# Local attention scores and value weighing on 64-row halves of the array, in a fused four-block network

## What is computed

```python
def local_attention(q, k, v):            # 16 heads of 64, windows of 32 tokens
    bk2, bv2 = (look(bk), look(bv))      # the window before and the own one: 64 keys
    sim = einsum('bhwie,bhwje->bhwij', bq, bk2) * QK_SCALE
    sim = where(mask, -finfo.max, sim)
    attn = softmax(sim, -1)
    out = einsum('bhwij,bhwje->bhwie', attn, bv2)
def ffn_layer(x, g, bln, W1, b1, W2, b2):
    hg = layernorm(x, g, bln) @ W1 + b1
    a, gate = split(hg, 2, -1)
    return a * gelu(gate) @ W2 + b2
for i in range(6):
    x = attn_layer(shift_tokens(x), ...) + x    # l2norm and rotary of q and k, output by Wo
    x = ffn_layer(shift_tokens(x), ...) + x
```

## Time and profile before

| | |
|---|---|
| three executions | 2566.87 to 2575.82 us, median 2572.84 |
| the profiled execution, its own time | 2572.18 us |
| its span, first to last instruction | 2570.4 us |
| stage 2 in the span | about 165.75 to 1949.57 us |
| one step of stage 2, steady | 36.48 us, the same within 0.02 us from step 5 on |
| busy shares of the span | PE 92%, DVE 69%, ACT 63%, POOL 62% |
| mean granted TensorE clock | 0.967 |

### The profile page before, as it was taken

One profiled execution on the slowest core, in us unless ns is written; L12 is line 12 of the kernel. 1 busy time (PEld: TensorE's weight loads), 2 busy tenths in 40 slices (PEclk: granted clock), 3 DMA queues, 4 the chain that ended last, 5 costly groups with the idle time before them and its releaser, 6 DMA issues.

```text
span 2570.4 us, 57541 instructions
## 1 busy us (share of the span) xinstructions
PE 2377.1 (92%) x22655; PEld 1629.8 (63%) x22655; DVE 1767.5 (69%) x2708; ACT 1615.4 (63%) x3162; POOL 1603.1 (62%) x931
## 2 busy tenths in 40 slices
PE   5669999999999999999999999999997888889998
PEld 3435666666666666666666666666665666656665
DVE  2348778777777777777877787778764888843232
ACT  1227777777777777777777777777773666643332
POOL 1039888888888888888888888888862222201111
PEclk8879999999999999999999999999997999989999
DMA  4002223322233222322232222322223000000000
GB/s 108 0 14 62 53 59 73 72 62 58 62 80 71 55 60 68 75 62 59 56 80 70 60 55 64 78 68 56 56 54 100 1 1 2 1 1 5 5 4 5
DMA packets 77196, 127.11 MB, mean 49 GB/s; under 512 B 24948, under 2 KB 48770, under 8 KB 76930
## 3 DMA queue, kind: packets, MB, share of 16 engines
q1 hardware_dynamic: 76930, 123.42, 20.6%
HBM read 26.56 MB, written 1.07 MB: 11 GB/s over the span
## 4 chain that ended last, share of the span: by engine, by line
PE 61%; DVE 13%; ACT 13%; issue 9%; POOL 3%; SPq 0%; DMA 0%; ACTq 0%; POOLq 0%; DVEq 0%
PE bank L527 8%; PE bank L563 7%; PE bank L604 7%; PE obank L584 6%; PE bank L618 6%; PE bank L813 5%; DVE qk L1211 2%; PE bank L538 2%; PE obank L823 2%; PE bank L823 2%; ACT kT L926 2%; ACT kT L925 2%; DVE mx L1367 2%; DVE sh L1364 2%; PE lnbank L548 2%
## 5 line engine op out<-in xcount | busy, mean ns | idle before, releaser
L1211 DVE TENSOR_TENSOR qk<-bank,tab 128x1024 f32<-128x1024 f32 x384 | 468.9, 1221 | 247.6 <-ACT qk L900 247.6
L1521 POOL TENSOR_TENSOR qk<-qk 128x1024 f32<-128x1024 f32 x192 | 454.3, 2366 | 251.9 <-DVE qk L1211 251.9
L1525 POOL TENSOR_TENSOR rn<-n2m,cst 128x16 f32<-128x16 f32 x192 | 562.5, 2930 | 16.0
L527 PE MATMUL bank<-wqk,xs 128*128 128x512 f32 x768 | 399.8, 602 | 4.0 <-DMA xs<-Z 1.3
L1529 POOL TENSOR_TENSOR qk<-qk,rn 128x1024 f32<-128x1024 f32 x192 | 365.2, 1902 | 28.1 <-POOL rn L1525 0.9
L900 ACT ACTIVATE qk<-bank 128x512 f32<-128x512 f32 x384 | 228.4, 595 | 210.0 <-PE bank L527 208.4
L538 PEld LDWEIGHTS bank<-cst,qk 128*128 128x128 f32 x1536 | 192.2, 141 | 210.6 <-issue 186.4
L1533 POOL TENSOR_TENSOR lnr<-lnv,cst 128x2 f32<-128x2 f32 (+1 forms) x88 | 66.2, 753 | 382.1 <-DVE lnv L1105 382.1
L538 PE MATMUL bank<-cst,qk 128*128 128x128 f32 x1536 | 231.7, 274 | 7.5 <-POOL qk L1529 7.5
L1218 DVE TENSOR_REDUCE n<-qk 128x16 f32<-128x1024 f32 x192 | 232.1, 1209 | 0.0
L912 ACT COPY vp<-lnbank 64x512 f32<-64x512 f32 x384 | 224.8, 585 | 9.4
(11 more groups left out here) (195 smaller groups left out, 4432.5 us busy)
## 6 DMA issues: line engine op xcount, KB each, us to landing
vp<-vp SPq DMA_DIRECT2D x672, 130.0 KB, 2.4
wqk<-in_L_ffn_Wqkv SPq DMA_DIRECT2D x24, 256.0 KB, 3.1
wv<-in_L_ffn_Wqkv SPq DMA_DIRECT2D x6, 512.0 KB, 3.6
wo<-in_L_ffn_Wo SPq DMA_DIRECT2D x6, 512.0 KB, 4.2
xs<-Z SPq DMA_DIRECT2D x48, 64.0 KB, 2.0
xs<-Z SPq DMA_DIRECT2D x48, 63.8 KB, 2.0
kT<-rel_by_distance SPq DMA_DIRECT2D x1, 2048.0 KB, 8.0
vp<-in_L_ffn_w SPq DMA_DIRECT2D x1, 2048.0 KB, 13.6
```

What stands on the lines that cost most here:

```text
L527: nc.tensor.matmul(bank[s % 2][:, :], xs[:, odd, WIN + r * P:WIN + r * P + P], wqk[:, lo:lo + 512], start=True, stop=True).then_inc(p_full, 1)
L1211: tt(qk[:, both, :].rearrange("p o (h d) -> p o h d", d=DH), heads(bank[c % 2][:, :]).unsqueeze(1).broadcast_to([P, 2, PAIRS, DH]), table. ...
L1521: tt(direct, direct, swapped, ALU.add).then_inc(sum_done, 1)
L1525: tt(rn[:, m % 2, :], n2m[:, :], const("mhalf"), ALU.pow).then_inc(rn_done, 1)
```

## The change

- `scores` and `weigh` work on the two 64-row halves of the array: for each head pair, window and half there is one matmul of 64 contraction rows and 32 stationary columns against 64 (scores) or 65 (weigh) columns. 32 matmuls in place of 16, and each half writes its own bank (`sbank` has two, `obank` has two).
- kT and vp lose their zero halves; ACT copies keys and values with one 128-row instruction in place of two of 64 rows. The memsets at the start and the spreading DMAs move half the bytes.
- `weigh` and `divide_out` move from the even slot to the odd slot after it, `divide_out` ahead of `norms`. `turn_out` and `take_out` move from the odd to the next even slot (the fourth one into slot 0 of the next step); `turn_out` now writes `obank[:, 1]`. `turn_probs` becomes the last operation of PE's odd slot. `seed` follows `shift_scores` at once.
- All three `hidden` blocks use bank 2, so block c waits for `gate` of block c-1.
- Stage 3's bias moves to two tiles, and stage 4's second weight gets a tile of its own.

```diff
-HD_BANK = (2, 4, 2)
...
-                    sp.wait_ge(v_done, 8 * t + 2)
+                    sp.wait_ge(v_done, 4 * t + 1)
...
                 for q in range(4):
                     for w in range(4):
                         lo = r * P + w * WIN
-                        keys = kT[:, 4 * g + q, :, lo:lo + 2 * WIN].rearrange("p o (s j) -> p o s j", s=2)
-                        mm = nc.tensor.matmul(s[WIN * w:WIN * w + WIN, q * P:q * P + P], qT[:, 4 * g + q, lo:lo + WIN],
-                                              keys if w % 2 else keys[:, :, ::-1, :], start=False, stop=True,
-                                              skip_group_check=True)
+                        for o in range(2):
+                            own = slice(64 * o, 64 * o + 64)
+                            keys = kT[own, 4 * g + q, lo:lo + 2 * WIN].rearrange("p (s j) -> p s j", s=2)
+                            mm = nc.tensor.matmul(sbank[WIN * w:WIN * w + WIN, o, q * DH:q * DH + DH],
+                                                  qT[own, 4 * g + q, lo:lo + WIN],
+                                                  keys if w % 2 else keys[:, ::-1, :], start=False, stop=True,
+                                                  skip_group_check=True)
...
                 wait(pe, ao_done, 4 * i + k)
+                wait(pe, ot_done, 4 * i + k)
                 for q in range(4):
                     for w in range(4):
-                        mm = nc.tensor.matmul(obank[WIN * w:WIN * w + WIN, q // 2, (q % 2) * VB:(q % 2) * VB + VB],
-                                              pT[:, k % 2, q * P + w * WIN:q * P + w * WIN + WIN],
-                                              vp[:, 4 * r + w, 4 * g + q, :], start=True, stop=True)
+                        for o in range(2):
+                            own = slice(64 * o, 64 * o + 64)
+                            mm = nc.tensor.matmul(obank[WIN * w:WIN * w + WIN, o, q * VB:q * VB + VB],
+                                                  pT[own, k % 2, q * P + w * WIN:q * P + w * WIN + WIN],
+                                                  vp[own, 4 * r + w, 4 * g + q, :], start=True, stop=True)
...
             def turn_out(i, k):
                 pe.wait_ge(ao_done, 4 * i + k + 1)
-                wait(pe, ot_done, 4 * i + k)
...
-                    mm = nc.tensor.transpose(bank[4][:, q * P:q * P + P], ao[:, k % 2, q * P:q * P + P], ident)
+                    mm = nc.tensor.transpose(obank[:, 1, q * P:q * P + P], ao[:, k % 2, q * P:q * P + P], ident)
...
-                if c == 2:
-                    pe.wait_ge(h_done, 3 * i + 1)
+                else:
+                    pe.wait_ge(h_done, 3 * i + c)
...
-                    if s % 2 == 0 and p1:
+                    if s in (2, 4, 6) and p1:
+                        turn_out(i, s // 2 - 1)
+                    if s == 0 and p2:
+                        turn_out(f, 3)
+                    if s % 2 == 1 and p1:
                         weigh(i, s // 2)
...
+                    if s in (1, 3, 5) and p1:
+                        turn_probs(i, s // 2 + 1)
+                    if s == 7 and p0:
+                        turn_probs(t, 0)
...
-                for o in (1, 0):
-                    lo = 64 * o
-                    src = vbank[lo:lo + 64, :].rearrange("p (a d) -> p a d", d=DH)
-                    cols = slice(o * (DH + 1), o * (DH + 1) + DH)
-                    nc.scalar.copy(vp[lo:lo + 64, 2 * j + 1, :, cols], src).then_inc(v_done, 1)
+                nc.scalar.copy(vp[:, 2 * j + 1, :, 0:DH], vbank[:, :].rearrange("p (a d) -> p a d", d=DH)).then_inc(v_done, 1)
...
-                    nc.scalar.copy(kT[0:64, pairs, 0, lo:lo + P], src[0:64])
-                    last = nc.scalar.copy(kT[64:P, pairs, 1, lo:lo + P], src[64:P])
+                    last = nc.scalar.copy(kT[:, pairs, lo:lo + P], src)
...
                     if s in (0, 2, 4) and p1:
                         shift_scores(i, s // 2 + 1)
+                        seed(i, s // 2 + 1)
...
+                    if s % 2 == 1 and p1:
+                        divide_out(i, s // 2)
                     if s % 2 == 1 and p0:
                         norms(t, s // 2)
```

More of the change, by code:

```diff
@@ L33 @@
 NE, EF = 8, 512
-VB = 2 * (DH + 1)
+VB = DH + 1
 KW = WIN + S
@@ L88, in sem @@
             return ctx.enter_context(nc.semaphore(name))
-        bank = [ctx.enter_context(nc.psum_tensor(f"bank{i}", [P, 512], F32)) for i in range(5)]
+        bank = [ctx.enter_context(nc.psum_tensor(f"bank{i}", [P, 512], F32)) for i in range(3)]
+        sbank = ctx.enter_context(nc.psum_tensor("sbank", [P, 2, 512], F32))
+        bank += [sbank[:, 0, :], sbank[:, 1, :]]
         obank = ctx.enter_context(nc.psum_tensor("obank", [P, 2, 512], F32))
@@ L175, in build @@
         bout = sb("bout", [P, 1])
-        bias = kTf[:, 0:H * S].rearrange("p (h t) -> p h t", h=H)
+        tabf = tab[:, :, :, :, :].rearrange("p l k r d -> p (l k r d)")
+        bias = [f[:, 0:PAIRS * S].rearrange("p (h t) -> p h t", h=PAIRS) for f in (kTf, tabf)]
         relv = sb("relv", [WIN, H])
@@ L395, in _ @@
             sp.wait_ge(o_full, 4 * ITEMS)
-            sp.dma_start(bias, bass.AP(relu_dram.ap().tensor, 0, [[1, P], [384, H], [1, S]])).then_inc(rel_in, 16)
+            sp.wait_ge(parts_done, 8 * ITEMS)
+            for half in range(2):
+                sp.dma_start(bias[half], bass.AP(relu_dram.ap().tensor, half * PAIRS * 384, [[1, P], [384, PAIRS], [1, S]]))\
+                    .then_inc(rel_in, 16)
             sp.dma_start(mw1, a["L1_ffn_w1"].rearrange("e m f -> m e f")).then_inc(ld_s4, 16)
@@ L544, in values @@
                     pe.wait_ge(ld_v, (i // B) * 16 + 16)
-                wait(pe, v_done, 8 * i + 2 * w)
+                wait(pe, v_done, 4 * i + w)
                 for o in range(2):
@@ L571, in turn_probs @@
                 for q in range(4):
[L572 removed]
+                    mm = nc.tensor.transpose(obank[:, 0, q * P:q * P + P], px[:, k % 2, q * P:q * P + P], ident)
                 mm.then_inc(pt_full, 1)
@@ L611, in hidden @@
                     pe.wait_ge(ld_w1, (i // B) * 16 + 16)
-                if c == 1:
-                    wait(pe, ot_done, 4 * i + 4 + min(3, 4 * (ITEMS - 1 - i)))
-                if c == 2:
-                    pe.wait_ge(h_done, 3 * i + 1)
+                else:
+                    pe.wait_ge(h_done, 3 * i + c)
                 n = P if c < 2 else FFR
                 for half in range(2):
-                    mm = nc.tensor.matmul(bank[HD_BANK[c]][0:n, half * S:half * S + S], w1[:, half * FF + c * P:half * FF + c * P + n],
+                    mm = nc.tensor.matmul(bank[2][0:n, half * S:half * S + S], w1[:, half * FF + c * P:half * FF + c * P + n],
                                           lnt[:, S:2 * S], start=True, stop=True)
@@ L649, in step @@
                         values(i, 3, 1 - odd)
-                    if s % 2 == 1 and p1:
-                        turn_out(i, s // 2)
-                    if s in (1, 3, 5) and p1:
-                        turn_probs(i, s // 2 + 1)
-                    if s == 7 and p0:
-                        turn_probs(t, 0)
                     if s == 0 and p2:
@@ L668, in step @@
                         contract(f)
+                    if s in (1, 3, 5) and p1:
+                        turn_probs(i, s // 2 + 1)
+                    if s == 7 and p0:
+                        turn_probs(t, 0)
             pe.wait_ge(masks_cast, 1)
-            nc.tensor.matmul(bank[3][:, :], ident_bf, maskv[:, 0, :], start=True, stop=True).then_inc(seeded, 1)
+            nc.tensor.matmul(bank[3][:, :], ident_bf, maskv[:, 0, :], start=True, stop=True)
+            nc.tensor.matmul(bank[4][:, :], ident_bf, maskv[:, 0, :], start=True, stop=True).then_inc(seeded, 1)
             step(0, 0, True, False, False, False)
@@ L980, in step @@
                         take_values(i, s // 2 + 2)
-                    if s % 2 == 1 and p1:
-                        take_out(i, s // 2)
+                    if s in (2, 4, 6) and p1:
+                        take_out(i, s // 2 - 1)
+                    if s == 0 and p2:
+                        take_out(f, 3)
                     if s in (0, 2, 4) and p1:
@@ L1363, in attend @@
                 part = sh[:, m % 2, :].rearrange("p (h n) -> p h n", n=w)
-                tt(part, bank[3 + m % 2][:, :].rearrange("p (h n) -> p h n", n=w), bias[:, hs[0]:hs[-1] + 1, S - w:S]
-                   if r == 0 else bias[:, hs[0]:hs[-1] + 1, :], ALU.add).then_inc(s3["add"], 1)
+                lo = hs[0] % PAIRS
+                tt(part, bank[3 + m % 2][:, :].rearrange("p (h n) -> p h n", n=w), bias[hs[0] // PAIRS][:, lo:lo + len(hs), S - w:S],
+                   ALU.add).then_inc(s3["add"], 1)
                 dve.wait_ge(s3["add"], NJ * b + m + 1)
```

61 lines of the change are left out of this document (28 added, 33 removed).

## The result

The change makes the kernel slower: median 2601.45 us of four executions (2597.34 to 2602.49), beside 2573.01 us for the kernel before on the same chip. The ratio is 1.0113, 95% interval 1.0101 to 1.0125. The profiled execution took 2602.49 us, its span is 2600.6. I had forecast 2599. Times are medians of all executions of a kernel; in experiment 6 alone one of the four, 7030.42 us, is left out as disturbed.

The account below looks back on a forecast made before the run. PE bounds the kernel before; the change adds a two-slot chain through the division. Steps go from 36.48 to 36.91 us, +19 over some 45, plus fill 2 and drain about 2; sum +23 to +27, 2599 us against the median, range 2510 to 2650.

Parts of the forecast that it names:

- The chain of 8.06 us: Loop over two slots through PE, ACT and DVE, closed by turn_probs waiting for the division: 8.06 us against 7.53 before.
- Slots 4 and 5: Pair bound by the two-slot chain: 8.06 us, with PE standing still at turn_probs for 1.3.
- slots 2 and 3: Pair bound by the chain plus 0.12, as squares start later behind the norm's deviations: 8.18 us.
- Slots 6 and 7: Pair with the hidden blocks, GELU, exponential and division in its chain: 10.40 us, against 10.21 before.
- the wait of block 2 for gate 1: New wait in slots 6 and 7, after a GELU 1.26 us behind block 1: gate 0.47 plus 0.15.
- Slots 0 and 1: PE bounds slot 0 at 5.95 us, slot 1 takes 4.32: 10.27 against 11.21 before, a gain.
- The burst: 64 small passes of scores or weigh on PE in 0.45 us in place of 0.87, saving PE 2.8 us per step.
- rival 1: PE still sets the pace, 2.8 us gained: 33.7 us per step, 2446 us; chance 0.24 for all that ends faster.
- PE's waits: PE idle before turn_probs for DVE's ao, 4 to 5 us per step in slots 1, 3, 5, 7; busy some 32.
- Fill and drain: The step filling the pipeline adds 2 us; draining steps, where hidden blocks wait for each other's gates, about 2.
- The ACT copies: Eight fewer ACT copies of about 0.58 us per step, 4.6 us in all: slack off the chain, gaining nothing.
- Rival 2's first form: Row halves take turns on the array, 0.42 us more per burst: +0.6 us per step, 2625 us; chance 0.12.

Follow-up runs that it names:

- experiment 6: The change with each scores burst cut in two of 32 passes, turn_out in between: 2622.85 us, ratio 1.0191 to the kernel before.
- experiment 3: The change with turn_probs moved behind the projection and turn of the next even slot: 2528.87 us, ratio 0.9838 to the kernel before.
- experiment 7: The change with the exponential moved behind the next odd slot's squares and take_turned on ScalarE: 2535.28 us, ratio 0.9849 to the kernel before.
- experiment 1: The kernel before, full-height bursts and double copies kept, with every operation placed as in the change: 2630.58 us, ratio 1.0230 to the kernel before.
- experiment 10: The placement of experiment 8 with full-height bursts and double copies, as in the kernel before: 2604.36 us, ratio 1.0133 to the kernel before.
- experiment 5: The change with ScalarE's copies of keys and values again in two instructions of 64 rows: 2611.22 us, ratio 1.0146 to the kernel before.
- experiment 8: The change with both the later turn_probs of experiment 3 and the later exponential of experiment 7: 2519.94 us, ratio 0.9788 to the kernel before.
- experiment 4: The change with weigh and division back in even slots, turn_out and turn_probs in odd; row halves stay: 2563.91 us, ratio 0.9969 to the kernel before.
- experiment 2: The change with VectorE doing the division ahead of parts in odd slots: 2624.94 us, ratio 1.0211 to the kernel before.
- experiment 9: Experiment 8 with POOL's root for the FFN norm moved ahead of rotate(0)'s last multiplication: 2543.65 us, ratio 0.9899 to the kernel before.
- experiment 12: Experiment 8 with the FFN norm's product written to PSUM (bank 2): 2519.62 us, ratio 0.9798 to the kernel before.
- experiment 11: Experiment 9 with the FFN norm's product written to PSUM (bank 2): 2516.65 us, ratio 0.9788 to the kernel before.

## Why the prediction was right, and where it was not

**The chain of 8.06 us** is what the change does. Slots 4 and 5 take 8.09 (forecast 8.06), slots 2 and 3 8.22 (8.18). Experiments 3 and 7 break it in two different places, on PE and on ScalarE, and either gives back 66 to 73 us; experiment 1 has it with other bursts. Shown.

**Slots 6 and 7**: 10.20, forecast 10.40. The step that failed is the wait of block 2 for gate 1: block 1's GELU came 1.06 behind it, not 1.26, the gate was done at 923.61, and PE was busy with scores and turn_out until 923.80. Block 2 so started 0.15 earlier than forecast, and its own GELU came 1.06 behind it, not 1.13. One bank for the FFN blocks cost nothing here. The 1.26 was a row in which ScalarE had other work first.

**Slots 0 and 1**: 10.49, forecast 10.27. Slot 0 is PE's own work, 6.13 for 5.95, and there the longer burst counts in full: scores with the way in and out took 0.22 more than forecast, turn_out 0.06 more and the output projection 0.10 less. Slot 1 is 4.36 for 4.32. That the sum of the four pairs was off by only 0.1 is luck in part: -0.20 in slots 6 and 7 and +0.22 in slots 0 and 1 cancel.

**The burst** was the term that was mis-sized: 0.45 us forecast, 0.64 from first to last start. The starts of 7 ns in the earlier trace rows were right, for four and for 32, but the kernel before starts the 32 passes of a burst over 0.81 us, a few at 7 ns and longer distances between them, so nothing in it could show what 64 do at that pace. PE saves 0.23 per burst where both are in the same places (experiment 10), 1.84 per step and not 2.8. For the time it hardly mattered outside slot 0, because PE waited anyway; it would have been the first error of rival 1. The rule of the Trainium skill on start to start, about 25 ns, "TensorE: Matmul & The Clock Gate", the back-to-back issue gap, is not what this trace shows for small tiles: 10 ns on average and 7 to 8 at first.

**PE's waits**: I expected 4 to 5 us a step for `ao` and PE busy for 32. It was 1.76 us in the three marked rows, with 0.60 for POOL's root, which I had not foreseen, and none in slot 1; PE was busy for 34.64. The 32 did not even follow from my own terms, 35.98 - 2.8 = 33.2. The sum of the slots was right since slots bound by the chain don't ask how long PE works; the split between work and waiting was wrong with the burst.

**Fill and drain**: +2 and +2 forecast; the fill came to +1.8 (-0.95 + 3.2 - 0.5) and the end to +5.2. The steady steps gave +0.53 for +0.43, some 4.5 us over 45 steps. So 30.3 us between the two profiled executions, for 26. The terms of the forecast, 19, 2 and 2, add up to 23; for the 3 us more in 2598 it has no term, and they brought it nearer by luck.

**The ACT copies** were called free. By experiment 5 they are worth 0.15 us a step, 7 us in all.

**Rival 1** (PE still sets the pace) is what experiments 3, 7 and 8 reach with the chain broken, at 2520 to 2535 us; its 2446 was out of reach with bursts of 0.64: it needs a step of 33.7, and in experiment 8 PE is busy for 34.44. Rival 2's first form (the halves take turns, 0.42 more per burst) was wrong in the cause and twice too large: a burst took 0.19 more, and experiment 6 shows halves that pack well for 32 passes.

**What the change as a whole is worth**: the places alone +58 us, the row halves and the single copies -29 together, by the steady steps some 21 and 7. Moving one transpose and one exponential turns it into a gain of 2.1%.

## What to carry to other kernels

Work saved on the busiest engine becomes time only where that engine doesn't wait: row halves and single copies together gave 29 us with a hand-over chain of 8.06 us per pair of slots around them, and 84 with the chain opened. When a wait is moved into the slot of its producer, write down the whole loop through every engine, start to start. Then move the waiting instruction behind the one that opens the next round (experiment 3), or the last link behind the first of the next round (experiment 7). And look at the engine that is next in line (POOL here) before freeing the first: two of these experiments lost more behind it than they had gained.

## Not expected of the hardware

- 32 passes of 64 rows by 32 columns start 7 to 8 ns apart, the following 32 some 12 ns apart; cut in two bursts, both halves are fast (0.24 us each), and a burst directly behind another starts fast again (33 passes in 0.30 us, experiment 4). With 128 passes in a row PE's stream broke off 51 times in 1500 us, by up to 1.8 us, with no releaser in the profile.
- Between small tiles and full size PE loses 0.09 us on the way in and 0.15 on the way out (experiment 6).
- VectorE's multiply-and-add from SBUF to SBUF (128 x 256 float32) takes 0.41 us where it meets only the last 0.16 us of a full-width product on POOL, and 0.79, 0.80, 1.50 or 1.76 where it meets more of it (before, experiments 8, 2 and 9), then ending some 0.15 behind that product. With a PSUM source it takes 0.54 or 0.55 with POOL's product beside it all the while (experiments 12 and 11). The Trainium skill has it so, "SBUF — State Buffer", "Who interferes with whom": of VectorE in its two-port mode and GpSimd the second to issue is fully blocked until the first has finished. The trace agrees (1.76, and 926.40 to 926.54); that this instruction ran in the two-port mode is inferred from it. VectorE's other products beside POOL kept their length here, 1.22 for parts and 0.69 for the division, both with a PSUM operand, and so did the sum of the squares, 1.21, which reads SBUF alone (experiment 8, from 912.13, POOL's product from 911.99 to 914.35). So an SBUF source by itself does not make an instruction wait.
- Stages 3 and 4, the same instructions in experiments 5, 8 and 11 and in the change, took 617.2 us at a mean granted clock of 0.94 and 624.0 at 0.92. Differences of a few us between kernels are better read from the steady steps.
